# TensorE's order within an attention group: transposes, scores, side piece, value products

## What is computed

```
q, k, v = heads(x @ Wq), heads(x @ Wk), heads(x @ Wv)
w = softmax(einsum('bhqd,bhkd->bhqk', q, k) / DH + causal)
w = w * mask
w = w / (sum(w) + 1e-8)
out = einsum('bhqk,bhkd->bhqd', w, v) @ Wo
x = x + out
```

## Time and profile before

| | |
|---|---|
| median of 3 runs | 3856.89 us |
| profiled execution | 3857.66 us, span 3855.9 us |
| PE busy | 3504.2 us (91%) |
| PEld (weight loads) busy | 3151.9 us (82%) |
| DVE busy | 3002.8 us (78%) |
| ACT busy | 2365.9 us (61%) |
| POOL busy | 820.8 us (21%) |
| granted clock of PE | 0.98 of 2.4 GHz |
| DMA | 37.1% of 16 engines' time in the main queue |

### The profile page before, as it was taken

One profiled execution on the slowest core, in us unless ns is written; L12 is line 12 of the kernel. 1 busy time (PEld: TensorE's weight loads), 2 busy tenths in 40 slices (PEclk: granted clock), 3 DMA queues, 4 the chain that ended last, 5 costly groups with the idle time before them and its releaser, 6 DMA issues. The chain is left out here.

```text
span 3855.9 us, 90130 instructions
## 1 busy us (share of the span) xinstructions
PE 3504.2 (91%) x29924; PEld 3151.9 (82%) x29924; DVE 3002.8 (78%) x4884; ACT 2365.9 (61%) x5622; POOL 820.8 (21%) x830
## 2 busy tenths in 40 slices
PE   0899996999999899989989998998999999599998
PEld 0899995888788788878878887887888888499998
DVE  7899984777777777777777777777777777599996
ACT  1454543676677667667767766776776777344544
POOL 2223221111122112112211211221121121123232
PEclk8999998999999999999999999999999999799999
DMA  6111114444534444444434444444444444211110
GB/s 211 63 55 52 54 36 129 102 102 105 130 96 118 103 116 111 108 119 99 121 97 116 114 110 114 98 119 100 116 114 102 110 109 109 92 40 51 57 49 34
DMA packets 162617, 374.13 MB, mean 97 GB/s; under 512 B 19696, under 2 KB 61552, under 8 KB 161776
## 3 DMA queue, kind: packets, MB, share of 16 engines
q1 hardware_dynamic: 162288, 370.30, 37.1%
HBM read 129.31 MB, written 39.58 MB: 44 GB/s over the span
## 5 line engine op out<-in xcount | busy, mean ns | idle before, releaser
L1233 ACT ACTIVATE at_eT_hi<-at_t_ps 128x512 f16<-128x512 f32 (+3 forms) x1536 | 745.3, 492 | 564.4 <-PE at_t_ps L1145 520.2
L1314 DVE SCALAR_TENSOR_TENSOR at_eT_lo<-at_t_ps,at_eT_hi 128x512 f16<-128x512 f32 (+3 forms) x1536 | 826.1, 551 | 163.0 <-ACT at_eT_hi L1233 132.6
L1225 ACT ACTIVATE at_e_rows<-at_s_ps,at_neg_max 128x1024 f32<-128x1024 f32 (+7 forms) x1024 | 767.0, 749 | 127.2 <-DVE at_neg_max L1308 126.3
L1145 PE MATMUL at_t_ps<-at_ident,at_e_rows 128*128 128x128 f32 x4608 | 778.8, 278 | 52.0 <-DVE at_eT_lo L1314 46.6
L1308 DVE TENSOR_REDUCE at_neg_max<-at_s_ps 128x1 f32<-128x1024 f32 (+7 forms) x1024 | 766.6, 749 | 41.8 <-PE at_s_ps L1135 30.4
L1131 PE MATMUL at_s_ps<-at_kh_st,at_q_st 128*128 128x512 f32 (+2 forms) x1536 | 581.1, 378 | 52.3 <-issue 25.4
L1159 PE MATMUL at_o_ps<-at_v_cols,at_eT_hi 128*128 128x130 f16 x4608 | 608.1, 221 | 19.0 <-ACT at_o_raw L1241 17.5
L1145 PEld LDWEIGHTS at_t_ps<-at_ident,at_e_rows 128*128 128x128 f32 x4608 | 503.6, 141 | 90.8 <-DVE at_eT_lo L1314 67.3
L1159 PE MATMUL at_o_ps<-at_v_cols,at_eT_lo 128*128 128x65 f16 x4608 | 566.8, 192 | 0.0
L1132 PE MATMUL at_s_ps<-at_kl_st,at_q_st 128*128 128x512 f32 (+2 forms) x1536 | 515.1, 343 | 0.0
L1159 PEld LDWEIGHTS at_o_ps<-at_v_cols,at_eT_hi 128*128 128x128 f16 x4608 | 434.0, 98 | 35.7 <-ACT at_o_raw L1241 21.7
(11 more groups left out here) (184 smaller groups left out, 7336.7 us busy)
## 6 DMA issues: line engine op xcount, KB each, us to landing
at_kh_st<-at_k_hi SPq DMA_DIRECT2D x256, 256.0 KB, 4.4
at_kl_st<-at_k_lo SPq DMA_DIRECT2D x256, 256.0 KB, 5.9
at_w_qk<-w_qk_split SPq DMA_DIRECT2D x65, 512.0 KB, 6.2
at_q_st<-at_q_hi SPq DMA_DIRECT2D x128, 256.0 KB, 3.9
at_q_st<-at_q_lo SPq DMA_DIRECT2D x128, 256.0 KB, 4.9
at_w_v<-w_v_split SPq DMA_DIRECT2D x66, 256.0 KB, 5.7
at_w_out<-w_out_split SPq DMA_DIRECT2D x64, 256.0 KB, 5.7
ffn_x_rows<-in_L_attn_query_dram SPq DMA_DIRECT2D x32, 256.0 KB, 2.8
```

The lines of the kernel that those rows point to most:

```text
L1145: last = nc.tensor.transpose(t_ps[i % 2][:, b * P:(b + 1) * P], e_rows[:, n % 4, (k0 + b) * P:(k0 + b + 1) * P], ident[:])
L1225: nc.scalar.activation(e_rows[:, n % 4, :w], s_ps[n % 2][:, col:col + w], ACT.Exp, bias=neg_max[:, n % 4:n % 4 + 1], accum_out=e_sum[:, pa ...
L1233: nc.scalar.activation(eT[0][:, i % EBUF, :count * P], t_ps[i % 2][:, :count * P], ACT.Copy, scale=PSCALE).then_inc(sem("eT_hi"), 1)
L1314: nc.vector.scalar_tensor_tensor(out=eT[1][:, i % EBUF, :count * P], in0=t_ps[i % 2][:, :count * P], scalar=PSCALE, in1=eT[0][:, i % EBUF, ...
```

## The change

Within a group PE had [scores of the unit after next], transposes, value products, [side piece], and now has transposes, [scores], [side piece], value products. Since all engines read one list, ACT's order moves too: the copy of a side piece, which stood behind the copy out and the exp of its group, now stands ahead of them. DVE's order is the same as before. Lines behind the edit stand 4 earlier.

```diff
     for n in range(NU):
         more = n + 2 < NU or after
         unit = ((n + 2) % NU, (n + 2) // NU)
-        if more:
-            steps.append(("scores",) + unit)
         for i in [i for i, (m, _, _) in enumerate(GROUPS) if m == n]:
             first = GROUPS[i][1] == 0
-            flush(late_hi)
             steps.append(("turn", i, 0))
             if i or before:
                 steps.append(("lo", (i - 1) % NG, (i - 1) // NG))
             flush(late_lo)
             if first and more:
+                steps.append(("scores",) + unit)
                 steps.append(("max",) + unit)
+            for piece in slots[i]:
+                if piece:
+                    steps.append(piece)
+                    late_hi.append((piece[0] + "_hi",) + piece[1:])
+                    late_lo.append((piece[0] + "_lo",) + piece[1:])
+            flush(late_hi)
             if i >= LAG or before:
                 steps.append(("value", (i - LAG) % NG, (i - LAG) // NG))
...
             if rows and i >= ROWS_FROM:
                 steps.append(("norm_x", i - ROWS_FROM, 1))
-            for piece in slots[i]:
-
-                flush(late_hi)
-                flush(late_lo)
-                if piece:
-                    steps.append(piece)
-                    late_hi.append((piece[0] + "_hi",) + piece[1:])
-                    late_lo.append((piece[0] + "_lo",) + piece[1:])
         if more:
             steps.append(("exp",) + unit)
```

## The result

The changed kernel takes **4030.28 us** (median, 4029.52 to 4031.22), the kernel before in the same runs 3856.82. The ratio is **1.0451**, with a 95% interval of 1.0436 to 1.0466. The forecast was 3949 us, 2.4% slower, with a range of 3880 to 4010. So the direction was right, the size was not: 173 us came, 92 had been summed. The profiled execution spans 4028.2 us at a mean granted clock of 0.986 (before 0.98), so the clock is at most a small part of it. These stretches cost at most 7 us more than before (an estimate: the time of each, times what its clock lacks to 1.00).

A forecast was written before the change was run, and what follows sets the result against it. PE was taken as the bound in the middle of the attention, busy 470 of 500 us. From 3857.7 us, waits add 145 and cheaper neighbours save 53, less 0.8 for the median: 3949 us, range 3880 to 4010.

The forecast's parts named there:

- Part 2: The waits of PE: they grow from 140 us to 285 us in all, by 145 us.
- Place A: Transposes 11 in an even pair: PE waits for `eT_lo` behind a long max and loses 1.33 us, before 0.49.
- Transposes 23: In even pairs, the same sum as at Place A with a shorter max: a loss of 1.24 us.
- Place B: Exp(10), behind transposes 13: the side piece's copy now stands ahead of the copy out, and PE loses 1.15 us.
- Transposes 6: Wait for exp(4), late behind the side k piece: a loss of 0.76 us where nothing was lost before.
- Part 1: What PE's steps cost by the neighbour ahead: 110 us before, 57 us after, 53 us less.
- The term of value products behind scores: In Part 1, value products behind scores, 498 times: between 0 and 40 us, taken as 0.
- The strict rule: Rival: weight loads are hidden in any case, so neighbours bring no gain; 4002 us, chance 0.04.
- 14 pairs: First and last pairs of a sequence: given 3.6 us of waits each, a little under the mean, 50 us.
- Cheaper neighbours win: Rival: waits stay at 140 us, one wait paying for the next, and neighbours save 53; 3804 us, chance 0.08.
- half of the waits: Rival: the waits overlap and only half of their growth comes; 3877 us, chance 0.12.
- The clock: Rival: gaps pile up or the clock falls to 1.2 GHz in them, up to 267 us more, 4216 us; chance 0.03.

The follow-up runs named there:

- the first two experiments: Each half of the change alone against the kernel before: side piece ahead of value products, scores first, 3942.01 us; scores behind transposes, side piece last, 3928.15 us.

## Why the prediction was right or wrong

**The direction and Part 2 held.** The two mechanisms of the forecast are there, at the places named, and the first two experiments show each by itself, at 3942 and 3928 us. Place A lost 1.32 us (forecast 1.33). Transposes 23 lost 1.33 (1.24), 17 lost 0.22 (0.28), 20 lost 0.07 (0.08), and the wo piece behind it 0.17 (0.16). Place B lost 1.07 (1.15). Transposes 6 lost 0.85 (0.76), transposes 9 0.52 (0.46), and v's second late piece 0.79 (0.76). Those of an even pair are 5.6 us in sum, where 5.46 had been counted. Transposes 0 behind an odd pair lost 0.69, where 0.59 had been counted with the odd pair. Two small ones in an even pair had been overlooked: the second q piece starts 0.22 us late and value 11 0.13.

**What failed first is a sentence of Part 1:** "Scores ahead of a side piece, and a side piece ahead of value products, are long enough to cost nothing." For scores it is wrong, since they end with the mask, and what stands just ahead decides, not the length of the whole step. 447 side pieces now stand behind scores, at 0.075 each: 33 of the 53 us that Part 1 counted never existed. The first group of an even pair (scores, transposes, value 21 and a q piece) went from 3.14 to 3.08 us, 0.06 instead of the 0.13 that the forecast's terms give there. The term of value products behind scores, taken as 0, was right (four blocks still take 0.35 us). The strict rule of the Trainium skill ("TensorE: Matmul & The Clock Gate", Part 2: What happens when you issue a matmul), by which the next weights load while a matmul runs, does not make neighbours free here: the same matmul takes 0.31 or 0.23 us with different ones ahead, and the run with the mask moved says the same. With the sentence read as one load behind one matmul, the rows agree.

**The second miss is a term that was not there:** the wait at transposes 2, behind ACT's stop. The forecast followed an even pair in the timelines, and took ACT in an odd one to be as early. The stop was in the trace of before, 2.27 us long, and cost less there (0.37 us, not 0.87), since PE had 0.4 us more to do until transposes 2. Writing ACT's loop out took back 12 us.

**The third is that 14 pairs were set "a little under the mean".** The first and last pairs of a sequence grew by 2.4 us each, where 3.6 us of waits less the old ones and less Part 1 make 0.6. That is some 25 us. Nothing had been read in them. The trace has waits there that the middle pairs do not have or have shorter: ahead of transposes 11 PE is idle for 1.49 us in the first pair (before 0.66); in the last it is idle for 0.71 ahead of transposes 18 and 1.25 ahead of the third wo piece (before nothing and 0.57). The further stretches at a lower clock, 7 us at most, are in these pairs too.

**The fourth is a release.** PE had gone on 0.14 us behind the end of an exp; now it takes 0.22 (1475.60 to 1475.82). Both are also the medians over all waits for an exp, and 0.08 us more, 185 times, is 15 us over all. The scores write the bank that the exp has left, the transposes take `e_rows` itself as weights; that this makes the difference was not tested. The row of the one was used for the other.

The terms overlap a little (the 14 pairs also have side pieces), so it is better to add by kind of pair. Even pairs are 0.7 us over their forecast of 40.0, 25 times; pairs with r = 3 and 5 1.7 over 44.1, 16 times; those with r = 1 and the last pair of all 0.9, 9 times; the 14 others 1.8. That is 17 + 27 + 8 + 25 = 77 of the 81 us that were missing.

**The rivals.** None came true. "Cheaper neighbours win" and "half of the waits" needed one wait to pay for the next, and the two halves measured alone show that these waits hardly do. "The strict rule" gave 4002 us, nearer than the forecast, for a reason that the rows refute. The clock stayed at its level through the gaps of the middle pairs, up to 1.2 us. It did fall behind the stop of 3 us at the start of a sequence, in both kernels; the changed one there:

```profile
2434.00:2436.00 2.00, 1.35 (x6) 1.26 (x7) 0.56 (x1) 0.12 (x1) 0.00 (x0) 0.52 0.07 16
2436.00:2438.00 2.00, 2.00 (x8) 1.62 (x7) 0.79 (x1) 0.47 (x1) 0.00 (x0) 0.50 0.00 0
```

So the clock did fall, but what the change added by it is 7 us at most and not 267. The result lies 20 us above the range, because its upper end took in one doubtful term of Part 1 at a time, and held no allowance for pairs that had not been read.

**What the signs said.** `eT_lo` waits of some 100 us (129), exps some 95 (98), at the transposes; the copy out nearly gone (3.3); PE's share 88% in the middle, an even pair 40.7 us: these held, though the waits for `eT_lo` went past their mark. An odd pair at 45.8 us, not about 44, pointed at transposes 2. The first matmul of a side piece at 0.23 us failed, and leads to the first miss.

## What to carry to other kernels

Where several engines run one list in order, a step moved ahead on one engine delays what stands behind it on the others. Count from the common starting point how much work each has until they meet again; this gave the waits that were counted to within 0.1 us here; the ones not looked for were the misses. Moving the late steps forward on the engine that makes them late took back 30 us and 10 us of 173 and made it worse when done together: each step moved up pushed another one back, max an exp, exp a copy out. Work that fits into a wait is better put into the wait: moving five of the ten side pieces of even pairs gained 0.3% (interval 0.2 to 0.45), while the change and all seven other orders of the lists lost against the kernel before.

What a first matmul costs was set here by the one matmul just ahead of it. Look at the last instruction of a step, not at the step's length. And read each kind of pair in the trace before giving it the mean.

## What the runs showed of the hardware

- ACT stood still for 2.2 to 2.6 us where its loop over pairs goes back to its start, before and after the change, and nowhere else in the attention for over 1 us without a wait. Written out, the same two instructions followed each other within 0.17 us. PE stood still for 2.8 to 3.4 us where its loop over sequences goes back (five times in each kernel), and not at its loop over pairs.
- The granted clock fell to the lower level (0.55 and 0.59 over 4 us) behind 1.55 us in which PE did nothing (run with two late maxima), and was back at 1.00 in the next stretch. Behind the 3.4 us at the start of a sequence it was 0.52, 0.50 and 0.50 over 6 us. The gaps of up to 1.2 us in the middle pairs of the changed kernel had no such effect: none of their stretches of 2 us is below 0.95.
- PE's transposes, whose weights are made by an exp, start 0.22 us behind the exp's end when they wait for it; scores, which only write the bank that the exp has read, 0.14 us behind.
- Behind the bf16 mask of 128 columns the next fp32 matmul takes 0.08 us longer to the next start (0.31 for 0.23, 0.20 for 0.12), as it does behind value products of 65 f16 columns and behind fp32 transposes of 128; behind an fp32 matmul of 256 or 512 columns it does not. Behind transposes the last of them takes 0.08 less in turn, so that only the other two cost time.
